# Loading and norming the next chunk's rows early and in place, in a fused attention and MLP block

## The reference

```python
x = x + layernorm(attention(layernorm(x)))     # 16 heads of 128, causal, softmax, biases
x = x + layernorm(mlp(layernorm(x)))           # 2048 wide, out = (gelu(x Wg') * (x Wu')) Wd'
```

## Time and profile before

| what | value |
|---|---|
| median of 3 runs (lowest, highest) | 1577.87 us (1573.5, 1579.29) |
| profiled execution, its own time | 1580.88 us |
| its span, from the first to the last instruction | 1579.1 us |
| busy: PE, DVE, ACT, POOL | 98%, 68%, 62%, 45% |
| chunks 1 to 6 of the attention | 147 to 911 us |

### The profile page before, as it was taken

One profiled execution on the slowest core, in us unless ns is written; L12 is line 12 of the kernel. 1 busy time (PEld: TensorE's weight loads), 2 busy tenths in 40 slices (PEclk: granted clock), 3 DMA queues, 4 the chain that ended last, 5 costly groups with the idle time before them and its releaser, 6 DMA issues.

```text
span 1579.1 us, 25677 instructions
## 1 busy us (share of the span) xinstructions
PE 1549.9 (98%) x8160; PEld 1332.4 (84%) x8160; DVE 1071.8 (68%) x3088; ACT 981.7 (62%) x2449; POOL 711.2 (45%) x1069
## 2 busy tenths in 40 slices
PE   6999999999999999999999999999999999999998
PEld 5888888888888888888888888887888888888887
DVE  5666677677777778667767766756666566565665
ACT  6887667767776776777776776653444444444443
POOL 5774445445554545445544543333333333333333
PEclk9999999999999999999999999999999999999999
DMA  4653444444454354444444455481101101111001
GB/s 135 188 169 114 142 137 145 146 155 137 139 173 134 124 172 135 145 156 131 141 152 144 146 162 159 155 289 52 43 26 54 41 28 42 38 54 41 27 28 40
DMA packets 168375, 183.13 MB, mean 116 GB/s; under 512 B 17328, under 2 KB 139696, under 8 KB 168240
## 3 DMA queue, kind: packets, MB, share of 16 engines
q1 hardware_dynamic: 168240, 181.50, 36.0%
HBM read 102.26 MB, written 79.17 MB: 115 GB/s over the span
## 4 chain that ended last, share of the span: by engine, by line
PE 79%; DMA 7%; SPq 4%; DVE 4%; ACT 4%; issue 2%; POOL 1%; DVEq 0%
PE fbank L752 13%; PE fbank L754 13%; PE fbank L753 13%; PE obank L752 6%; PE obank L754 6%; PE obank L753 6%; PE ubank L752 5%; PE ubank L754 5%; PE ubank L753 5%; DMA turned_scratch<-turned 3%; PE ubank L776 3%; PE fbank L854 2%; SPq L524 2%; DMA back<-turned_scratch 2%; ACT probs L640 1%
## 5 line engine op out<-in xcount | busy, mean ns | idle before, releaser
L752 PE MATMUL fbank<-xnT_hi,wqk_hi 128*128 128x512 f32 x768 | 301.2, 392 | 1.1 <-DVE xnT_lo L932 1.1
L753 PE MATMUL fbank<-xnT_lo,wqk_hi 128*128 128x512 f32 x768 | 300.2, 391 | 0.0
L754 PE MATMUL fbank<-xnT_hi,wqk_lo 128*128 128x512 f32 x768 | 299.8, 390 | 0.0
L1327 POOL TENSOR_TENSOR pT_lo<-back,pT_hi 128x512 fp32r<-128x512 f32 x128 | 165.8, 1295 | 290.6 <-ACT pT_hi L708 290.6
L651 ACT ACTIVATE w_raw<-fbank 128x512 f32<-128x512 f32 x128 | 76.5, 598 | 230.6 <-PE fbank L754 230.5
L1289 POOL TENSOR_SCALAR probs<-probs,rsum 128x128 f32<-128x128 f32 (+1 forms) x512 | 208.8, 427 | 14.5 <-DVE rsum L955 10.5
L947 DVE CUSTOM_DVE_ANT_0 probs<-ubank,mask 128x128 f32<-128x128 f32 (+1 forms) x512 | 155.9, 355 | 25.3 <-PE ubank L754 24.1
L754 PEld LDWEIGHTS fbank<-xnT_hi,wqk_lo 128*128 128x128 f32 x768 | 144.7, 188 | 30.8
L752 PEld LDWEIGHTS fbank<-xnT_hi,wqk_hi 128*128 128x128 f32 x768 | 145.4, 189 | 28.7 <-DVE xnT_lo L932 1.5
L753 PEld LDWEIGHTS fbank<-xnT_lo,wqk_hi 128*128 128x128 f32 x768 | 145.0, 189 | 25.7
L1307 POOL TENSOR_TENSOR v_lo<-probs,v_hi 128x512 fp32r<-128x512 f32 x64 | 82.4, 1288 | 166.0 <-ACT v_hi L660 166.0
(11 more groups left out here) (144 smaller groups left out, 4288.4 us busy)
## 6 DMA issues: line engine op xcount, KB each, us to landing
turned_scratch<-turned SPq DMA_DIRECT2D x128, 384.0 KB, 2.6
back<-turned_scratch SPq DMA_DIRECT2D x512, 96.0 KB, 2.2
w_raw<-in_w_pairs SPq DMA_DIRECT2D x28, 256.0 KB, 3.0
w_hi_scratch<-w_hi SPq DMA_DIRECT2D x48, 128.0 KB, 2.0
w_lo_scratch<-w SPq DMA_DIRECT2D x48, 128.0 KB, 2.0
x_res<-in_x SPq DMA_DIRECT2D x16, 256.0 KB, 2.9
wqk_hi<-w_hi_scratch SPq DMA_DIRECT2D x16, 256.0 KB, 5.5
wqk_lo<-w_lo_scratch SPq DMA_DIRECT2D x16, 256.0 KB, 5.9
```

Of the source, the lines that this page charges most:

```text
L752: nc.tensor.matmul(out, a[0], b[0], start=start, stop=False, skip_group_check=skip)
L753: nc.tensor.matmul(out, a[0], b[1], start=False, stop=False, skip_group_check=skip)
L754: return nc.tensor.matmul(out, a[1], b[0], start=False, stop=stop, skip_group_check=skip)
L1327: pool.tensor_tensor(lo[:].rearrange("p u b (a j) -> p (u b) a j", j=32), mem.back[m % 2][:, :, 0:2].rearrange("p a u b j -> p (u b) a j") ...
```

## The change

The x loads move from steps 3 and 5 to step 15 of the chunk before (chunk 0: both to step 3). The rows are normed inside x_in, in steps 0 to 5 of the chunk (chunk 0: 5 to 8), and xT reads x_in; `stream` is left to x1 alone, so the norm no longer waits for the stored x1. VectorE's parts of x1 are spread over steps 4 to 13, some of them at a new place, "mid", between the values. SP's turn of the given rows moves from step 5 to step 7, both x1 stores to step 14. Slot 15 of the weight pieces goes: seven a chunk, and the last six pieces are made in chunk 7. In the first MLP chunk the given rows' parts come one tile later; the next rows' norm takes two tiles instead of four.

```diff
-W4_SLOTS = [1, 3, 5, 7, 9, 11, 13, 15]
-X1_ROOTS, NEXT_ROOTS = 9, 13
+W4_SLOTS = [1, 3, 5, 7, 9, 11, 13]
+X1_ROOTS, NEXT_ROOTS, FIRST_NEXT_ROOTS = 10, 2, 6
...
 def x1_norm(c):
-    return 2 * c + 2
+    return 2 * c + 3
...
 def next_norm(c):
-    return 2 * c + 3
+    return 2 * c + 2 if c else 3
...
+def stored_chunks(engine, s, chunks):
+
+    if chunks:
+        engine.wait_ge(s.first_stored, 32)
+    if chunks > 1:
+        engine.wait_ge(s.stored, 32 * (chunks - 1))
...
@@ load_program
-        sp.wait_ge(s.w4_stored, 32 * PIECES)
+        sp.wait_ge(s.w4_stored, 32 * (2 * unit + 2))
...
         if c:
-            sp.wait_ge(s.xn, c)
+            sp.wait_ge(s.full, nth(("xT", c, KT - 1)))
         else:
             sp.wait_ge(s.first_xn, TT)
         if c == NCH - 1:
-            sp.wait_ge(s.stored, 32 * (NCH - 2))
+            sp.wait_ge(s.first_stored, 32)
...
-        if c and j == 5:
+        if c and j == 7:
             turn_given(c - 1)
...
-        if j in (3, 5):
-            next_x(c, (j - 3) // 2)
-        elif c and j in (11, 13):
-            store_x1(c, (j - 11) // 2)
+        if c == 0 and j == 3:
+            for i in range(2):
+                next_x(c, i)
+        elif c and j == 14:
+            for i in range(2):
+                store_x1(c, i)
         elif j == 15:
+            for i in range(2) if c < NCH - 1 else ():
+                next_x(c + 1, i)
             load_res(c, 0)
...
@@ scalar_program, ahead of the last head's output
             act.wait_ge(s.out, m // HEADS + 1)
+            stored_chunks(act, s, m // HEADS)
...
@@ tensor_program
-            transpose_x(mem.stream, m, bank).then_inc(s.full, 1)
+            transpose_x(mem.x_in, m, bank).then_inc(s.full, 1)
...
@@ vector_program
             dve.wait_ge(s.rstd, next_norm(c))
-            if c:
-                dve.wait_ge(s.stored, c * 32)
-            last = standardise(xn, x_in, 2 * (part - 3))
+            last = standardise(x_in, x_in, 2 * (part - 3))
...
-    X1_AT = {(3, "sum"): (-2,), (4, "sum"): (-1,), (6, "sum"): (0,), (8, "sum"): (1, 2),
-             (9, "end"): (3, 4, 5, 6)}
-    NEXT_AT = {(10, "sum"): (0,), (12, "sum"): (1, 2), (13, "end"): (3, 4)}
+    X1_AT = {(4, "sum"): (-2,), (6, "sum"): (-1,), (8, "sum"): (0,), (9, "mid"): (1, 2),
+             (10, "sum"): (3,), (12, "sum"): (4,), (13, "mid"): (5, 6)}
+    NEXT_AT = {(0, "sum"): (0,), (1, "mid"): (1, 2), (2, "sum"): (3,), (5, "mid"): (4,)}
+    FIRST_NEXT_AT = {(5, "mid"): (0,), (5, "end"): (1, 2), (6, "sum"): (3,), (8, "sum"): (4,)}
...
             if whole(kind, m):
-                if m == TT - 1:
-                    extra(c, j, "end")
+                extra(c, j, "end" if m == TT - 1 else "mid")
                 continue
...
@@ between, MLP
-            for part in {4: (-1,), 7: (0, 1), 8: (2, 3), 9: (4, 5)}.get(m, ()):
+            for part in {4: (-1,), 8: (0, 1), 9: (2, 3), 10: (4, 5)}.get(m, ()):
...
-        if 7 <= j < 11 and c < NCH - 1:
-            norm_next_y(j - 7, c)
+        first = 7 if c else 9
+        if j in (first, first + 1) and c < NCH - 1:
+            for part in (0, 1):
+                norm_next_y(2 * (j - first) + part, c)
...
@@ pool_program, MLP
-            if m == (7 if c == 0 else 4):
+            if m == (8 if c == 0 else 4):
                 roots(y_norm(c))
-            elif j == 8 and c < NCH - 1:
+            elif j == (7 if c else 9) and c < NCH - 1:
                 roots(y_next_norm(c))
```

More of the change, by code:

```diff
@@ L340, in __init__ @@
         self.res_used = sem("residual_added")
+        self.first_stored = sem("first_x1_stored")
         self.stored = sem("x1_stored")
@@ L488, in store_x1 @@
         sp.dma_start(part_of(x1_v, c - 1, i),
-                     mem.stream[:, i * half:(i + 1) * half]).then_inc(s.stored, 16)
+                     mem.stream[:, i * half:(i + 1) * half]
+                     ).then_inc(s.stored if c > 1 else s.first_stored, 16)
     def load_res(c, i):
@@ L588, in finish_y @@
         sp.dma_start(mem.x_res[:], chunk(x1_v, c)).then_inc(s.yres, 16)
-    sp.wait_ge(s.stored, 32 * (NCH - 1))
+    stored_chunks(sp, s, NCH - 1)
     for c in range(NCH):
@@ L598, in load_program @@
             else:
-                sp.wait_ge(s.xn, NCH)
+                sp.wait_ge(s.full, nth(("xT", NCH, KT - 1)))
             sp.dma_start(mem.x_in[:], chunk(x1_v, c + 1)).then_inc(s.x, 16)
@@ L1047, in spread @@
                           ALU.bitwise_or).then_inc(s.spread, 1)
-    X1_AT = {(3, "sum"): (-2,), (4, "sum"): (-1,), (6, "sum"): (0,), (8, "sum"): (1, 2),
-             (9, "end"): (3, 4, 5, 6)}
-    NEXT_AT = {(10, "sum"): (0,), (12, "sum"): (1, 2), (13, "end"): (3, 4)}
+    X1_AT = {(4, "sum"): (-2,), (6, "sum"): (-1,), (8, "sum"): (0,), (9, "mid"): (1, 2),
+             (10, "sum"): (3,), (12, "sum"): (4,), (13, "mid"): (5, 6)}
+    NEXT_AT = {(0, "sum"): (0,), (1, "mid"): (1, 2), (2, "sum"): (3,), (5, "mid"): (4,)}
+    FIRST_NEXT_AT = {(5, "mid"): (0,), (5, "end"): (1, 2), (6, "sum"): (3,), (8, "sum"): (4,)}
     def extra(c, j, place):
+        for part in (NEXT_AT if c else FIRST_NEXT_AT).get((j, place), ()):
+            norm_next_x(part, c)
         for part in X1_AT.get((j, place), ()) if c else ():
             finish_x1(part, c)
-        for part in NEXT_AT.get((j, place), ()):
-            norm_next_x(part, c)
         piece = piece_of_step(c * HEADS + j)
@@ L1319, in pool_program @@
                 w4_lo(piece)
+            if j == (NEXT_ROOTS if c else FIRST_NEXT_ROOTS):
+                roots(next_norm(c))
             if c and j == X1_ROOTS:
                 roots(x1_norm(c))
-            if j == NEXT_ROOTS:
-                roots(next_norm(c))
         elif kind == "pT":
```

## The result

| | before | changed |
|---|---|---|
| median of all runs beside each other | 1578.6 us | 1607.0 us (1604.0 to 1607.5, 4 runs) |
| ratio, 95% interval | | 1.018 (1.015 to 1.021) |
| profiled execution's span | 1579.1 us | 1605.5 us |

The change made the kernel slower by 1.8%, where +0.25% and a range up to 1595 us were forecast. The profiled spans differ by 26.4 us, the medians by 28.4.

A forecast was written before the change was run, and what follows sets the result against it. TensorE was taken to bound the kernel, stalled in the attention by VectorE's splits and SP's single queue. Costs of 18.2 us less gains of 14.2 gave +4.0, so 1582 us (+0.25%), range 1570 to 1595.

The forecast's parts named there:

- the two rivals on that side: Slower: send(0) late behind step 15's loads, 1593 us, chance 0.20; clock falling at steps 8 to 10, 1594, 0.10.
- The given turn: SP's turn in step 7 makes step 8's send 3.5 us late, costing 2.1 in each of seven chunks: 14.7.
- 1.4 free, then each us costs one: Attention steps: 1.4 us of lateness in the probabilities' turn through HBM is free, each further us costs one.
- VectorE's wait: In step 9, VectorE stalls some 0.7 us for the given rows, counted as part of the 2.1 per chunk.
- The x loads: Both x loads in step 15, ahead of the residual's, delay the next send: 0.4 us seven times, 2.8 (0 to 17).
- 0.4, nearer to that row: Step 15: cost per chunk taken near a traced row where 768 KB, issued earlier, delayed a send 1.2 us.
- The x1 stores: Both x1 stores in step 14: SP on time, landing within the free 1.4 us, cost 0 (0 to 5).
- What goes away: Stalls removed in attention chunks 1 to 6 (7.9 us), chunk 7 (2.1) and the MLP's start (4.2): together 14.2 us.
- The stall of chunk 7: Chunk 7's step 5 weight loads start some 5 us before the next send, so its 2.1 us go.
- The MLP's start: After the attention, given rows' parts one tile later remove 2.5 us of gap and 1.7 of lowered clock: 4.2.
- The rival of the clock: Steps 8 to 10: if the 2.1 us come as one gap, the clock falls, 12 us more: 1594, chance 0.10.
- The faster rival: Given turn mostly hidden, 0 to 0.9 us of cost, and step 15 costs nothing: 1567 us, chance 0.17.

The follow-up runs named there:

- late_stats: On the changed kernel, given statistics moved from the end of step 8 to step 9's middle and end, SP's turn left in step 7: 1615.5 us.
- b_x15: On the kernel before, only the x loads moved, both halves to step 15 of the chunk before: 1585.6 us, ratio 1.0033.
- split_turn: On the changed kernel, given store kept in step 7, its four loads after step 8's fetch, given statistics in step 9: 1580.7 us.
- mlp_old: On the changed kernel, the MLP's part of the change undone: 1617.9 us, ratio 1.022.
- b_turn7: On the kernel before, SP's given turn moved from step 5 to 7, all given statistics at the end of step 8: 1607.6 us.

## Why the prediction was wrong

**The mechanism was right; two terms of the sum were too small, and one was put at zero.** The direction of the doubt was named (slower), and the two rivals on that side gave 1593 and 1594. The measured 1607 lies past both, since the first came true and more, the clock's came true in part, and the main term was short as well. By the step sums the costs were 41.2 us where 18.2 were forecast (24.6 and 16.6), and the gains 14.9 where 14.2 were.

- **The given turn, 14.7 us forecast (6 to 24), measured 24.6**, or 22.0 over what these steps lost before. The step that failed is "SP is free at 4.6 + 4.6 = 9.2, the send of step 8 was due at 6.9: 2.3 late". Step 8's send left 4.2 us after scores(9) on the mean, 3.7 late, so 1.4 later than that. The larger part, 0.9, is the first 4.6. It is a clean step's, but in the changed kernel the given store left 4.8 to 6.6 us after scores(8), 5.5 on the mean, since step 7's own send left as late as 1.1 us after the scores and landed after as much as 3.4. Chunk 7, with scores(8) at 992.63, is the worst:

```profile
993.73 0.40 SPq L523 DMA_DIRECT2D turned_scratch<-turned  x1
996.99 2.14 SPq L533 DMA_DIRECT2D back<-turned_scratch  x4
999.23 0.38 SPq L542 DMA_DIRECT2D given_scratch<-w_raw  x1
1002.22 1.73 SPq L546 DMA_DIRECT2D w_raw<-given_scratch  x4
```

  Another 0.3 is the store's landing, 2.86 us in the row that was used; the seven turns of before took 2.8 to 4.2, those of the changed kernel 2.9 to 4.1 (mean 3.2). With 1.0 for the send's own landing the lateness is 4.7 and not 3.5. By the rule "1.4 free, then each us costs one" that is 3.3 a chunk, 23 us, against the 21.1 that are left when the clock's falls are taken off: the rule itself held. The quickest row of each leg should not have stood for the mean.
- **VectorE's wait, forecast at 0.7 as a part of it, was 2.7** (19.2 over seven). The given rows were back 6.5 us after scores(9) on the mean, not 5.2, and VectorE asked at 3.8, not 4.4. That it is a part of the same account was right (late_stats).
- **The x loads, 2.8 forecast (0 to 17), measured 8.3 alone (b_x15), and 16.3 together with the x1 stores.** The forecast put "0.4, nearer to that row": it trusted a row in which 512 of the 768 KB were issued 3.4 us ahead of the send, and in the changed kernel all of them are within 1.6 us. The number by bytes, 1.1 a chunk or 7.7 us, was in the text and is what b_x15 measures. The Trainium skill (DMA: Bandwidth & Descriptors, "Anatomy of one DMA") gives, as an estimate, 1.8 us of delay for 768 KB, or 5.6 us in all. The trace of b_x15 has 2.1 on the mean (4.1 to 5.0 us against 2.4), a little more than the page.
- **The x1 stores, forecast 0, cost 6 to 8.** "On time, and the landing stays within the free 1.4" failed in three of the six chunks that have stores: send(15) left up to 1.4 us late and landed after 3.0 to 4.5 us, 2.1 to 2.2 late in all, and j=1 lost 2.7. What was not followed at all is that a late fetch(15) also starts the x loads late, and send(0) with them: it leaves 2.0 us after the scores in four of those six chunks, where 0.5 is due, and 0.1 us after the loads are issued.
- **What goes away was right.** 10.0 forecast for the attention without the MLP: the other steps fell by 8.6, and split_turn has 0.3 left of j=9's 2.1. The stall of chunk 7 is gone, as is every wait of xT. The MLP's start was to give 4.2 and gave 2.0 (3.1 by mlp_old): the fall of the clock went, but VectorE still stood 1.6 us for the given rows, because SP issued their store 31.7 us after scores(15) of chunk 7 and not 29.6.
- **The rival of the clock** had 0.10 and 12 us. In the changed kernel the clock fell three times, 5.1 us in all, twice where the rival had it; in b_turn7, with gaps of 2.9 to 3.7 us, it came true whole. Its "one case" was not the only one of the kernel before: there is a fall in chunk 0 too (next section).
- **The faster rival** is spoken against by every run with the whole turn in step 7.

## What to carry to other kernels

A DMA queue issued in program order is an engine with a schedule of its own: before moving a transfer, above all one whose landing the queue waits for, count what must still leave between it and the next critical send, and move it only to where the consumers have slack (here the steps with value matmuls) or cut it so that the queue doesn't wait. When TensorE waits for a vector engine's split, follow that engine's own idle time one step further back: the DMA behind it was the cause, and spreading vector work evenly brought its gain only once the queue had been put right. Price such a move with the mean of the rows over all chunks, also for the legs that stay as they are, and carry lateness through to the next step, as slack can be spent once.

## What the runs showed of the hardware

- **The length of one gap doesn't tell whether the granted clock falls.** Before, it fell to the lower level around a gap of 2.28 us and, in chunk 0, around one of 2.01 at 37.62. In the changed kernel there are three falls in the attention (at about 479, 947 and 1008 us), around gaps of 1.77 us at 477.99, 1.92 at 945.79 and 2.81 at 1008.41; gaps of 1.81, 1.84, 1.89, 2.01 (at 217.67) and 2.36 us (at 742.77) had none. Windows of the changed kernel, a long one whose mean is still 1.00, and two in which the level of 1.2 GHz was granted for a while:

```profile
40.00:480.00 440.00, 428.94 (x2421) 374.46 (x2420) 305.11 (x1029) 315.98 (x870) 227.54 (x379) 1.00 0.45 144
480.00:500.00 20.00, 19.69 (x102) 16.59 (x101) 12.52 (x44) 12.80 (x34) 9.01 (x16) 0.94 0.35 111
...
1000.00:1020.00 20.00, 17.19 (x82) 14.64 (x81) 11.08 (x42) 10.86 (x31) 7.34 (x14) 0.91 0.57 186
```

  The mean of 0.91 over 20 us is 1.8 us lost. What decides, these runs leave open.
- **Issuing a store sometimes holds the queue.** In chunk 1 the given store took SP 1.49 us to issue in the changed kernel (at 207.43) and 1.55 in split_turn, which has another of 1.31 in chunk 5. In the six other turns of the changed kernel it took 0.38 to 0.46, as in step 5, and all of them stand right behind four fetches. Why was not tried.
